# Cross attention: TensorE adds the causal mask to both diagonal blocks, and all masked keys come back as one exponent per row

## The reference, cut to what matters

```python
scores = jnp.einsum('bhqd,bhkd->bhqk', qh, kh) / math.sqrt(hd)
causal = ki <= qi
scores = jnp.where(causal[None, None], scores, -10000.0)
attn = jax.nn.softmax(scores, axis=-1)
out = jnp.einsum('bhqk,bhkd->bhqd', attn, vh)
...
x = x + jnp.tanh(g_xattn[1]) * out
```

## Time and profile before

| | |
|---|---|
| median of 3 executions | 2247.9 us (2247.34 to 2250.03) |
| profiled execution, its own time | 2249.69 us |
| its span, first to last instruction | 2247.9 us |
| mean granted TensorE clock | 0.963 of full speed |
| PE busy over the span | 1996.2 us (89%) |
| DVE busy | 1371.1 us (61%) |
| ACT busy | 1073.3 us (48%) |
| POOL busy | 425.4 us (19%) |

### The profile page before, as it was taken

One profiled execution on the slowest core, in us unless ns is written; L12 is line 12 of the kernel. 1 busy time (PEld: TensorE's weight loads), 2 busy tenths in 40 slices (PEclk: granted clock), 3 DMA queues, 4 the chain that ended last, 5 costly groups with the idle time before them and its releaser, 6 DMA issues. The chain is left out here.

```text
span 2247.9 us, 33557 instructions
## 1 busy us (share of the span) xinstructions
PE 1996.2 (89%) x10802; PEld 1531.6 (68%) x10818; DVE 1371.1 (61%) x2400; ACT 1073.3 (48%) x2593; POOL 425.4 (19%) x504
## 2 busy tenths in 40 slices
PE   6999479999989999987997999999689979997898
PEld 5888357776767677766886778778578866665454
DVE  6777266666666666663323764554544328885786
ACT  3333156666656666653113412121134318885898
POOL 1111034444444444430000000000000001222110
PEclk9999789999999999998998999999899989998999
DMA  5665662323232321006443221112295322321111
GB/s 213 243 243 231 244 178 76 98 64 103 60 101 76 85 76 48 22 27 239 145 136 137 83 75 38 56 37 57 62 339 198 118 81 68 113 94 48 48 56 43
DMA packets 192217, 250.42 MB, mean 111 GB/s; under 512 B 11574, under 2 KB 143814, under 8 KB 181836
## 3 DMA queue, kind: packets, MB, share of 16 engines
q1 hardware_dynamic: 192076, 248.67, 33.9%
HBM read 152.14 MB, written 96.48 MB: 111 GB/s over the span
## 5 line engine op out<-in xcount | busy, mean ns | idle before, releaser
L930 ACT ACTIVATE at_prob<-at_S,at_bias,at_rq 128x384 f32<-128x384 f32 (+1 forms) x256 | 184.2, 731 | 165.3 <-DVE at_bias L1016 159.1
L1027 DVE TENSOR_TENSOR at_pt_lo<-at_PT,at_pt_hi 128x512 fp32r<-128x512 f32 x224 | 148.8, 688 | 92.6 <-ACT at_pt_hi L937 92.6
L798 POOL TENSOR_SCALAR at_prob<-at_prob,at_rsum 128x384 f32<-128x384 f32 (+1 forms) x256 | 160.3, 639 | 174.7 <-DVE at_rsum L1022 174.7
L1444 ACT ACTIVATE gu_silu<-gu_G 128x512 f32<-128x512 f32 x64 | 38.3, 598 | 269.6 <-PE gu_G L103 260.1
L857 PE MATMUL at_PT<-c_ident,at_prob 128*128 128x128 f32 x896 | 127.8, 277 | 44.1 <-DVE at_pt_lo L1027 44.1
L937 ACT ACTIVATE at_pt_hi<-at_PT 128x512 fp32r<-128x512 f32 x224 | 127.9, 604 | 53.1 <-PE at_PT L857 53.1
L1007 DVE TENSOR_REDUCE at_nmax<-at_S 128x1 f32<-128x384 f32 (+1 forms) x256 | 147.7, 615 | 4.7 <-PE at_S L850 4.2
L857 PEld LDWEIGHTS at_PT<-c_ident,at_prob 128*128 128x128 f32 x896 | 97.7, 140 | 75.6 <-DVE at_pt_lo L1027 71.2
L1477 DVE TENSOR_TENSOR gu_h<-gu_silu,gu_U 128x512 f32<-128x512 f32 x64 | 43.9, 687 | 154.6 <-PE gu_U L103 109.7
L846 PE MATMUL at_S<-at_k_hi,at_q_hi 128*128 128x384 f32 (+1 forms) x256 | 112.7, 440 | 16.6 <-DVE at_q_lo L1032 13.4
L789 POOL TENSOR_TENSOR at_rq<-at_qv,c_minus_half 128x4 f32<-128x4 f32 x64 | 65.1, 1017 | 288.0 <-DVE at_qv L1002 288.0
(11 more groups left out here) (272 smaller groups left out, 5658.5 us busy)
## 6 DMA issues: line engine op xcount, KB each, us to landing
wide<-at_ot SPq DMA_DIRECT2D x64, 256.0 KB, 2.9
wide<-gu_h SPq DMA_DIRECT2D x64, 256.0 KB, 3.2
o_a<-wide SPq DMA_DIRECT2D x14, 1024.0 KB, 4.8
d_a<-wide SPq DMA_DIRECT2D x14, 1024.0 KB, 4.8
keys_hi<-kv_kt_hi SPq DMA_DIRECT2D x8, 1024.0 KB, 4.0
keys_lo<-kv_kt_lo SPq DMA_DIRECT2D x8, 1024.0 KB, 6.0
values_hi<-kv_v_hi SPq DMA_DIRECT2D x8, 1024.0 KB, 8.0
values_lo<-kv_v_lo SPq DMA_DIRECT2D x8, 1024.0 KB, 9.6
```

The source lines that it names most:

```text
L798: pool.tensor_scalar(prob[u % 2][:, h, 0:n], prob[u % 2][:, h, 0:n], rsum[:, s:s + 1], 1.0, ALU.mult, ALU.mult).then_inc(normed.sem, 1)
L930: act.activation(prob[u % 2][:, h, 0:n], S[h][:, 0:n], ACT.Exp, bias=bias[:, s:s + 1], scale=rq[u % 4][:, h:h + 1], accum_out=sums[:, s:s ...
L1027: dve.tensor_tensor(pt_lo[f % 4][:], bank_of("p", u, kb)[:], pt_hi[f % 4][:].bitcast(F32), ALU.subtract).then_inc(pt_done.sem, 1)
```

## The change

What it does, part by part:

- **Mask on PE.** `scores` gets two more matmuls for each pair, one for each head: the bf16 identity as weights and a bf16 mask (0 or -1e30), read twice, as the moving operand, 256 columns, added to both diagonal blocks. `copy_predicated` is gone. A masked score is now about -1e30, its exponent 0.
- **Bound on the maximum.** The quarter of S with -10000 still bounds query block 0. For query block 1 the bound comes from a new `tensor_scalar` (minimum with `bound`) on the 128x4 result.
- **Masked keys as one term, for both query blocks.** `exps_apart` covers 2 x 16 columns instead of 16. The number of masked keys of a row (`count`) multiplies it instead of 128, in two instructions. The sum of masked values is now a matmul with a triangular matrix `later`: step 1 has two matmuls of 512 columns (`later` on values block 0, ones on values block 1), step 2 has one (`later` on values block 1). DVE copies M twice. The first copy must be done before the second matmul.
- **POOL** multiplies and adds for both query blocks: two more instructions for each batch, the first pair of them in step 2.
- **Start.** DVE makes the tables from one more loaded matrix (8 small instructions), and PE waits for them before its chain.

```diff
-                pool.tensor_tensor(xe[:], x[:, QT * b, :], ev[:], ALU.add).then_inc(xe_done.sem, 1)
+                pool.tensor_tensor(xe[:, t, :], x[:, n, :], ev[:], ALU.add).then_inc(xe_done.sem, 1)
...
-                if i == 3:
+                if i in (2, 3):
                     for a in batch(-1):
-                        add_apart(*a)
+                        add_apart(*a, i - 2)
...
-            def second_values(turn, b):
-
-                pe.wait_ge(*cx_arrived[b].at(turn, 16))
-                pe.matmul(M[:], c.ones[:], cx[:, QT * b + 1, :], start=True, stop=True).then_inc(V1_full.sem, 1)
+            def masked_values(turn, b, t):
+
+                if t == 0:
+                    pe.wait_ge(*cx_arrived[b].at(turn, 16))
+                    pe.wait_ge(*x_kept[1].at(turn, b + 1))
+                else:
+                    pe.wait_ge(*vm_kept.at(turn, QT * b + 1))
+                last = pe.matmul(M[:], later[:], cx[:, QT * b + t, :], start=True, stop=(t == 1))
+                if t == 0:
+                    last = pe.matmul(M[:], c.ones[:], cx[:, QT * b + 1, :], start=False, stop=True)
+                last.then_inc(VM_full.sem, 1)
...
                 for a in range(2):
-                    last = pe.matmul(S[p % 2][:, 2 * L * a + L:2 * L * (a + 1)], qt[b][rows[a], k, P:L],
-                                     kt[b][rows[a], k, :], start=True, stop=True)
+                    pe.matmul(S[p % 2][:, 2 * L * a + L:2 * L * (a + 1)], qt[b][rows[a], k, P:L],
+                              kt[b][rows[a], k, :], start=False, stop=False)
+                for a in range(2):
+                    diagonals = S[p % 2][:, 2 * L * a:2 * L * (a + 1)].rearrange("p (t l) -> p t l", t=QT)[:, :, 0:P]
+                    last = pe.matmul(diagonals, c.ident_bf[:],
+                                     mask[:].rearrange("p (a l) -> p a l", a=1).to_broadcast([P, QT, P]),
+                                     start=False, stop=True)
                 last.then_inc(S_full.sem, 1)
...
-                if i == 1:
-                    for turn, b in batch(0):
-                        pe.wait_ge(*x_kept[1].at(turn, b + 1))
-                        second_values(turn, b)
+                if i in (1, 2):
+                    for a in batch(0):
+                        masked_values(*a, i - 1)
...
+            pe.wait_ge(tables, 7)
             chain(pe, step)
...
-                wait_apart(dve, S_full, turn, p + 1, passed)
-                dve.copy_predicated(bank[:, :, 0:P],
-                                    after[:].rearrange("p (a l) -> p a l", a=1).to_broadcast([P, 2 * QT, P]),
-                                    masked[:].rearrange("p (a l) -> p a l", a=2 * QT)).then_inc(masked_done.sem, 1)
-                dve.wait_ge(*masked_done.at(turn, p + 1))
-                dve.tensor_reduce(nmax[:, 2 * p:2 * p + 2, :], bank, AX_X, ALU.max, negate=True).then_inc(max_done.sem, 1)
+                own = nmax[:, 2 * p:2 * p + 2, :]
+                dve.wait_ge(*S_full.at(turn, p + 1))
+                dve.tensor_reduce(own, bank, AX_X, ALU.max, negate=True).then_inc(seen_done.sem, 1)
+                dve.wait_ge(*seen_done.at(turn, p + 1))
+                dve.tensor_scalar(own, own, bound[:, 0:1], None, ALU.min).then_inc(max_done.sem, 1)
...
-                dve.scalar_tensor_tensor(out=sums[:, QT * b, :], in0=apart[:], scalar=float(P), in1=sums[:, QT * b, :],
-                                         op0=ALU.mult, op1=ALU.add).then_inc(sums_done.sem, 1)
+                for t in range(QT):
+                    last = dve.scalar_tensor_tensor(out=sums[:, QT * b + t, :], in0=apart[:, t, :], scalar=count[:, t:t + 1],
+                                                    in1=sums[:, QT * b + t, :], op0=ALU.mult, op1=ALU.add)
+                last.then_inc(sums_done.sem, 1)
...
+                if i in (1, 2):
                     for a in batch(0):
-                        keep_second_values(*a)
+                        keep_masked_values(*a, i - 1)
                 if i == 2:
                     for turn, b in batch(1):
                         ln.statistics(dve, turn, b)
```

More of the change, by code:

```diff
@@ L1567, in cross @@
         gain = mem.sb("gain", [P, TT, H1])
-        apart = mem.sb("apart", [P, H1])
-        apart_gain = mem.sb("apart_gain", [P, H1])
-        v1 = [mem.sb(f"v1_{b}", [P, D]) for b in range(2)]
+        apart = mem.sb("apart", [P, QT, H1])
+        apart_gain = mem.sb("apart_gain", [P, QT, H1])
+        vm = [mem.sb(f"vm{b}", [P, QT, D]) for b in range(2)]
         ev = mem.sb("ev", [P, D])
-        xe = mem.sb("xe", [P, D])
+        xe = mem.sb("xe", [P, QT, D])
         ot = mem.sb("ot", [P, DC, L])
@@ L1576, in cross @@
         after = mem.sb("after", [P, P], I32)
-        masked = mem.sb("masked", [P, 4 * P])
+        after_f = mem.sb("after_f", [P, P])
+        later = mem.sb("later", [P, P])
+        mask_f = mem.sb("mask_f", [P, P])
+        mask = mem.sb("mask", [P, P], BF16)
+        count = mem.sb("count", [P, QT])
+        bound = mem.sb("bound", [P, 1])
+        masked = mem.sb("masked", [P, 1])
         S = [mem.bank(f"S{i}", (P, 1024)) for i in range(2)]
@@ L1611, in cross @@
         masks = mem.sem("masks")
+        tables = mem.sem("tables")
         passed = mem.sem("passed")
@@ L1724, in _ @@
         def _(pe):
-            for s in (X_full, V1_full, S_full, PT_full, PV_done, O_turned):
+            for s in (X_full, VM_full, S_full, PT_full, PV_done, O_turned):
                 s.start(pe)
@@ L1892, in _ @@
         def _(dve):
-            for s in (x_kept[1], v1_kept, masked_done, max_done, sums_done, rsum_done, gain_done, apart_gained, o_done,
+            for s in (x_kept[1], vm_kept, seen_done, max_done, sums_done, rsum_done, gain_done, apart_gained, o_done,
                       ln.stats, ln.xn_ready):
@@ L1899, in _, with make_tables @@
             dve.wait_ge(masks, 3)
-            dve.wait_ge(setup, 16)
+            def make_tables():
+                dve.wait_ge(setup, 2 * 16)
+                dve.tensor_copy(mask[:], mask_f[:]).then_inc(tables, 1)
+                dve.tensor_copy(after_f[:], after[:]).then_inc(tables, 1)
+                dve.wait_ge(tables, 2)
+                dve.tensor_tensor(later[:], after_f[:], c.ident[:], ALU.add).then_inc(tables, 1)
+                dve.tensor_reduce(count[:, 1:2], after_f[:], AX_X, ALU.add).then_inc(tables, 1)
+                dve.wait_ge(tables, 4)
+                dve.tensor_scalar(later[:], later[:], -1.0, 1.0, ALU.mult, ALU.add).then_inc(tables, 1)
+                dve.tensor_scalar(count[:, 0:1], count[:, 1:2], float(P), None, ALU.add).then_inc(tables, 1)
+                dve.tensor_scalar(bound[:], count[:, 1:2], 0.5, 3e38, ALU.is_lt, ALU.mult).then_inc(tables, 1)
+                dve.wait_ge(tables, 7)
+                dve.tensor_scalar(bound[:], bound[:], -MASKED_L1, None, ALU.max).then_inc(tables, 1)
+                dve.wait_ge(tables, 8)
             def keep_x(turn, b):
```

52 lines of the change are left out of this document (27 added, 25 removed).

## The result

| | before | changed |
|---|---|---|
| median | 2248.97 us (4 runs) | 2268.72 us (4 runs) |
| profiled execution | 2249.69 us | 2268.47 us |
| its span | 2247.9 us | 2266.7 us |

The ratio is 1.0091, 95% interval 1.0077 to 1.0105: slower by 17 to 24 us. The medians differ by 19.8 us. The forecast was 27.7 us, the rival with the cheaper mask pair 20.7 us.

The account below looks back on a forecast made before the run. PE's work and a PE-ACT loop bound all steps but DVE's step 6; six batches 19.4, first 2.75, last 3.74, start 0.4, tail 1.4 sum to 27.7 us, so 2275.6 us, range 2264 to 2288.

Parts of the forecast that it names:

- the rival with the cheaper mask pair: Mask matmuls on PE: only 0.11 us a pair, as the change-over hides one of the two; 7.0 us less, 2268.6; 15%.
- DVE's relief: DVE in step 6: earlier maxima cut 4.08 to 3.57 us, 0.51 us in each of six batches; nothing elsewhere.
- What bounds the stage: Steps 0, 1, 2, 4 full of PE work, 5 and 7 on a PE-ACT loop, only step 6 set by DVE.
- Mask pair: Two bf16 matmuls a pair, in PE's content and the PE-ACT loop: 0.22 us, 1.76 us a batch.
- the change-over is only moved, not doubled: Reason for 0.22 us a mask pair: the change from 32-row to full-width matmuls, paid by the turned head today, only moves.
- Matmuls on M: One more 0.99 us matmul in each of steps 1 and 2: 1.98 us a batch, 0.99 in the first.
- Start, tail, first batch: One more DMA at the start 0.4 us; POOL's tail 1.4 us longer; first batch 2.75 us longer.
- The new waits of PE: PE waiting for DVE's first copy of M in step 2 and for the tables at the start: nothing.
- DVE sets the pace: Rival: ACT's 17.7 us of waits for DVE's maxima come back, PE's additions fall into gaps; 2232.0 us; 5%.
- The lock between DVE and POOL: Rival: POOL holds the new tensor_scalar, so steps 5 and 6 lengthen, about 1 us in seven batches; 2282.6 us; 13%.
- The dear mask pair: Rival: mask matmuls on PE take 0.42 us a pair, 12.8 us more, 2288.4 us; 12%.

## Why the prediction was right

The direction, the range and the place of the cost were right. The sum was 7 us too high: two of its terms were too dear, and a third, DVE's relief, was worth much less, while step 6 got its forecast length for another reason.

**What bounds the stage.** Right. PE's work, and a loop of scores, odd head, copy and exponents, set seven of eight steps. Only step 1 was read a little wrong: it was the loop's (3.05 us), with 0.04 us of wait for ACT in it, and not full of PE work. The forecast's reading that DVE was the one that waits was borne out by the run without the predicated copy: 48.7 us of work removed, 3.1 us of time. What the forecast didn't see is how near DVE was behind: as soon as PE's steps got shorter (without fillers, without the mask pair) it held steps 4 to 6.

**Mask pair: right in place, too dear.** The pair takes the forecast 0.22 us, in front of both kinds of step. The term of the sum that was mis-sized rests on "the change-over is only moved, not doubled". It was not moved. Today's filler pays 0.1 us behind the 32-row matmuls; the bf16 pair doesn't pay it there, and the filler, now second, doesn't either. Net 0.13 us, 8.3 us for 64 pairs instead of 14.1. My lower case, 0.11 us because the change-over hides one of the two, named what happened and its size within 0.02 us; I gave it 15%.

**Matmuls on M: right, 15% too dear.** 0.82 us net in step 1 and 0.85 in step 2, not 0.99. A distance between starts at the edge of the 32-row matmuls holds 0.1 us that is paid once, whichever matmul stands there: the added one takes 0.86. In step 1 PE's 0.04 us of wait for ACT went as well. About 2.3 us in all. The run without them gives 12.8 us for the term, where the forecast had 14.9.

**DVE in step 6: the length right by luck.** 4.08 fell to 3.84, and the forecast had 3.79 with the mask pair in it, by 0.51 us of relief. The row behind it, against the earlier trace rows:

```profile
1984.14 0.37 ACT L1865 ACTIVATE x_prob<-x_S,x_nmax 128x128 f32<-128x128 f32 x1 [0.88 <-DVE x_nmax L1954]
```

0.88 us of wait instead of 1.11. But the kernel before with the mask pair on top has the same step 6, 3.83 us, and the same 7.01 us of steps 5 and 6, with every predicated copy in place. Steps 4 to 6 together last 10.70 us before, 10.71 with the pair on top (1966.34 to 1977.05) and 10.72 now. So in this batch step 6 is shorter because steps 4 and 5 in front of it got longer while DVE took as long as ever, and DVE's relief is worth nothing. What the removed copy gave, 0.69 us ahead of the maximum of pair 5, went for the new `tensor_scalar` (0.23), for the hold by POOL just before the norm (some 0.15), and for the norm, which takes 2.50 us with POOL working beside most of it, instead of 2.28 before and 2.16 with the pair on top. By the same comparison the relief shows only in the second batch and the seventh, 0.5 and 0.4 us: under 1 us together, not 3.1. The sum didn't suffer, since the same two steps hide the mask pair, which the forecast had charged in full.

Steps 5 and 6 stay DVE's, at 7.02 us, just above PE's 6.89. In the kernel before, with the mask pair missing, and without the odd filler the two steps last 7.12 or 7.13. In steps 3 and 4 PE is the later one, as forecast, and the two last 6.89 us (3.19 and 3.70; forecast 7.1). It was close: ACT's exponents of pair 3 start 4.6 us after the scores of step 3, not 4.2.

**Start, tail, first batch.** The tail is 1.5 us longer (forecast 1.4). The first batch, from the first score to its `exps_apart`, grew from 32.4 to 34.4 us: 2.0, not 2.75, again the two prices. The start costs about 0.4 us: first score 14.2 us after the first load is issued, instead of 13.8. The new waits of PE show nowhere.

**The rivals.** "DVE sets the pace" fell with the run without the predicated copy. The lock between DVE and POOL is real and reaches the maximum of pair 5, but costs at most 0.13 us a batch, since PE's content stands just below; the rival had 1 us. (The instruction of the earlier trace rows ended 0.55 us after POOL's, not right after it: it was held, and then did its work.) The dear mask pair didn't come, and the cheap one did.

The sum with the measured terms: seven batches 15.4, the first 2.0, start 0.4, tail 1.5, together 19.3; the stages ahead happened to end 0.7 us earlier in the profiled execution, which leaves the 18.8 of its span within 0.2. By the experiments: mask pair 6.3, matmuls on M 12.8, start and tail 1.9, together 21.0 against 20.5, so that nothing of size is left for DVE's relief.

## What to carry to other kernels

Long waits for an engine don't mean that its work costs time: ask which step becomes shorter when that work is gone, and look at the steps' start times, not at the waits. Work moved from an engine with idle time onto one that fills its steps costs time in every such step, even at 0.2 us an instruction pair; the same matmul was free in a step that had a gap. When pricing from distances between starts, take off what the neighbours pay anyway at a change of shape. And a step that comes out as forecast doesn't prove the forecast's reason: here only the run with the mask pair alone showed that step 6 was shorter without any relief of DVE. Sum a chain over several steps before crediting one of them.

## What the runs showed of the hardware

- A 128x128 fp32 matmul takes 0.32 us to its follower right behind 32-row matmuls, and 0.23 behind full-width ones; a 128x512 one 0.86 us, and 0.95 right ahead of 32-row ones. Two bf16 matmuls of 256 columns took 0.22 us behind 32-row matmuls, and the fp32 one behind them 0.23, so that 0.22 us of work added 0.13. No run has the pair anywhere else.
- An instruction of 128x4 elements on DVE was shut out for the rest of a 1.05 us instruction on POOL: 0.23 us alone, 0.95 beside it. One that began 0.05 us before POOL's (at 2056.19) took its 0.23.
- Without the filler matmuls the granted clock fell to 1.2 GHz for 13 us once and for 17 us once, and more shortly a third time, though PE still looked busy over 80% of the stage in the profile; at half clock a step of 2.8 us took 4.8.
